# A routed mixture-of-experts block on one core: a table region per expert, slots ranked part by part, and the attention tile through the table

## The chip, the core and the metric

The kernel runs on one core of a Trainium2 chip. The metric is the device time of one execution in microseconds (us), here the median of three. In the profile, PE is TensorE (PEld its weight load), DVE VectorE, ACT ScalarE, POOL GpSimd, and SPq, ACTq, POOLq the queues of DMA-issuing or control instructions of an engine.

## What is computed

The input x has 8 sequences of 512 tokens of 256 numbers. A small attention touches only the first 16 tokens of each sequence (128 tokens in all); every token gets an output bias. Then every token goes through a router, its four best of 32 experts, and two shared experts.

```python
def reference(...):
    x = x + attn(layernorm(x))          # changes tokens 0..15 of each sequence, adds ob to all
    x = x + ffn(layernorm(x))
def ffn(tokens):                        # 4096 tokens of 256
    scores = sigmoid(tokens @ router_weight.T)             # 32 experts in 4 groups of 8
    sfc = scores + router_bias
    group_scores = top_k(grp, 2)[0].sum(-1)                # keep 2 groups, then 4 experts
    topk_w = scores[topk_idx]; topk_w = 2.5 * topk_w / topk_w.sum()
    out_e = (silu(tokens @ gate_w[e].T) * (tokens @ up_w[e].T)) @ down_w[e].T
    return sum_k(topk_w[k] * out_e[topk_idx[k]]) + shared(tokens)
```

Counting the router's choices over the given input: 16,384 pairs of a token and an expert lie on 17 experts and fill 136 tiles of 128 rows when every expert is rounded up; without the 128 attention tokens there are 15,872 pairs in 133 tiles.

## The kernel before

All in float32. Tokens lie in 32 tiles of 128: tile 0 holds the 128 attention tokens, tiles 1 to 31 the rest.

1. **Normalise and score.** DVE takes the statistics of groups of tiles (`statistics`, L1042), ACT normalises each tile (L572), PE turns it (`turn`, L730) and multiplies by the router's weights (`logits`). Turned tiles stay in SBUF as `xnT`, in the upper half of `gu_w`, where the weights of experts 16 to 31 will go.
2. **Route tiles 1 to 31** on DVE in two halves (`route_parts`, L1069): the chosen experts become a 0/1 array `hot`, PE counts with it, and DVE makes of the counts a slot in a table in DRAM for each pair. The slots of all experts are packed behind each other, each expert rounded up to 128, so a slot needs the total of every expert first.
3. **Attention** on tile 0: 23 steps that alternate between PE and DVE (`from_pe`, `to_pe`, `after_dve`), with the shared experts' work (`units`) put between them by the list `UNITS_AT`. Beside it ACT stages each tile four times with its pair numbers (`stage`, L591: 4 buffers in `xg`, so tile n waits until the rows of tile n - 4 have left), and POOL scatters four times 128 rows per tile to the table (L535), 124 times in all. `STAGE_AT` and `ADD_AT` say in which step ACT stages a tile and DVE adds a finished pair of shared-expert results to x. The table was blanked before by four DMAs of 5,140 KB (L398).
4. **Dense steps.** Tile 0 doesn't go through the table: 32 steps (`PLAN`, kind "dense") run all 32 experts over it, weighted by `w0`.
5. **Expert steps.** 134 steps (`FIXED`) load a tile of 128 rows of the table (L425, address known when the program is built), turn it (L922), gate and up (L946), turn the hidden values (L952), down (L970); POOL scatters the result to `pairs_dram` (L542). Expert numbers come from a small table read into PE registers. Steps beyond `FIXED` stand in branches that are taken only if more tiles are used (133 are).
6. **Combine.** SP loads the four results of each token (L457), DVE adds them with their weights (L1477), SP stores.

SP issues its DMAs in program order. The second half of the gate and up weights is the L418 entry below: it waits for the last `up` of the shared experts and for the 12th addition of `add_pairs`, since both still read `xnT`.

```python
            sp.wait_ge(up_done, SHARED)
            sp.wait_ge(pair_added, KEPT_IN_XNT)
            for m in range(2, 4):
                e = slice(8 * m, 8 * m + 8)
                sp.dma_start(gu_w[:, e], gate_up[:, e]).then_inc(gu_in[1], 16)
```

## Time and profile before

| | us |
|---|---|
| median of 3 runs (range) | 551.88 (550.71 to 553.16) |
| the profiled execution | 550.75 |
| its span, first to last instruction | 549.0 |
| PE busy (share of the span) | 418.3 (76%) |
| DVE, ACT, POOL busy | 280.3, 240.5, 287.9 |
| mean granted clock | 0.936 |

A row of the timeline has the start, the duration, engine, line, operation, output<-input and count, and in brackets the idle time before it and what ended it. A stretch view gives the busy time of each engine in a stretch, the granted TensorE clock as a share of 2.4 GHz, the DMA engines' share and GB/s. The chain of waits is followed back from the last instruction. All times of the trace count from the start of the span.

### The profile page before, as it was taken

To read this page: it belongs to the slowest core of one execution; us is meant where nothing else is said; L and a number is where in the kernel's file an instruction comes from. 1 tells how busy PE (TensorE), PEld (TensorE's weight loads), DVE (VectorE), ACT (ScalarE), POOL (GpSimd) and SP (SyncE) were. 2 spreads that over 40 slices of the span, in tenths; PEclk is the share of its full clock that TensorE was granted. 3 is DMA by queue.
4 is the path that set the end of the run, shared out by engine and by line. 5 is a ranking of instruction groups with operands and counts; after the bars stand their busy time and mean duration, and the time that the engine had idled before them with its cause. 6 is when DMAs were issued, how large, how long until landed. Compare 5 with 4: busy or idle time off the path is not lost.

```text
span 549.0 us, 8776 instructions
## 1 busy us (share of the span) xinstructions
PE 418.3 (76%) x2118; PEld 325.6 (59%) x2119; DVE 280.3 (51%) x997; ACT 240.5 (44%) x625; POOL 287.9 (52%) x421
## 2 busy tenths in 40 slices
PE   0699236898896976999999999999999999920000
PEld 0699114555453543888888888888888888810000
DVE  4967785764553434343366633223232322308997
ACT  0687501427644552422455555555555555510000
POOL 6430028886888888760166565656656565630000
PEclk9999998999998998999999999999999999985555
DMA  7999999532232373935055555455454454339996
GB/s 178 274 419 417 418 423 398 149 107 77 106 106 98 106 266 124 366 98 155 11 168 157 162 152 149 153 162 157 145 169 153 154 172 139 105 106 410 369 402 241
DMA packets 42549, 111.48 MB, mean 203 GB/s; under 512 B 7929, under 2 KB 25468, under 8 KB 38272
## 3 DMA queue, kind: packets, MB, share of 16 engines
q1 hardware_dynamic: 29824, 78.24, 41.5%
q0 software_dynamic: 12384, 32.59, 17.1%
q8 instruction: 23, 0.38, 0.3%
q14 instruction: 30, 0.25, 0.2%
q10 hardware_dynamic: 288, 0.03, 0.0%
HBM read 53.01 MB, written 59.13 MB: 204 GB/s over the span
## 4 chain that ended last, share of the span: by engine, by line
PE 53%; DVE 9%; ACT 2%; DMA 1%; issue 1%; SPq 0%; POOL 0%; POOLq 0%; ACTq 0%; DVEq 0%
PE two_banks L946 26%; PE two_banks L970 11%; DVE x_sb L1477 9%; PE two_banks L922 5%; PE two_banks L952 3%; PE two_banks L783 3%; PE two_banks L961 3%; PE two_banks L809 2%; DMA gu_w<-pairs_dram 1%; ACT L588 0%; ACT loopb L598 0%; DMA pairs_dram<-routing,loopb 0%; ACT routing L612 0%; PE two_banks L887 0%; PE two_banks L904 0%
## 5 line engine op out<-in xcount | busy, mean ns | idle before, releaser
L542 POOL DMA_INDIRECT pairs_dram<-routing,loopb x134 | 131.8, 984 | 112.0 <-issue 80.9
L535 POOL DMA_INDIRECT slots_dram<-loopb,slot_i x124 | 121.5, 979 | 70.6 <-DVEq L1267 41.8
L946 PE MATMUL two_banks<-gu_w,routing 128*128 x536 | 137.9, 380 | 0.0
L1439 DVE TENSOR_TENSOR routing<-routing,two_banks 128x128 f32<-128x128 f32 x134 | 38.6, 288 | 135.8 <-ACT routing L689 122.9
L946 PEld LDWEIGHTS two_banks<-gu_w,routing 128*128 128x128 f32 x536 | 91.5, 190 | 7.0
L970 PE MATMUL two_banks<-dn_w,routing 128*128 x268 | 80.0, 381 | 0.0
L684 ACT ACTIVATE routing<-two_banks 128x256 f32<-128x256 f32 x134 | 51.5, 384 | 64.9 <-PE two_banks L922 64.9
L783 PE MATMUL two_banks<-gu_w,sgu_w 128*128 128x512 f32 x128 | 64.8, 644 | 11.1 <-DMA sdn_w<-in_sh_down 5.5
L689 ACT ACTIVATE routing<-two_banks 128x128 f32<-128x128 f32 x166 | 46.1, 278 | 58.7 <-PE two_banks L946 58.7
L1477 DVE SCALAR_TENSOR_TENSOR x_sb<-gu_w,wts,x_sb 128x256 f32<-128x256 f32 x124 | 49.5, 480 | 12.7 <-DMA gu_w<-pairs_dram 12.6
L698 ACT ACTIVATE routing<-two_banks 128x256 f32<-128x256 f32 x134 | 50.6, 378 | 1.4 <-PE two_banks L970 1.3
L922 PE MATMUL two_banks<-ident,loopb 128*128 128x128 f32 x268 | 51.2, 273 | 0.0
L598 ACT ACTIVATE loopb<-x_sb,shift,rstd 128x1024 f32<-128x1024 f32 x31 | 38.2, 1233 | 27.4 <-DMA slots_dram<-loopb,slot_i 27.3
L1445 DVE COPY routing<-two_banks 128x128 f32<-128x128 f32 x166 | 47.1, 284 | 0.4 <-PE two_banks L952 0.2
L970 PEld LDWEIGHTS two_banks<-dn_w,routing 128*128 128x128 f32 x268 | 40.5, 191 | 10.3 <-issue 0.2
L783 PEld LDWEIGHTS two_banks<-gu_w,sgu_w 128*128 128x128 f32 x128 | 24.6, 205 | 36.9 <-issue 23.7
L922 PEld LDWEIGHTS two_banks<-ident,loopb 128*128 128x128 f32 x268 | 37.8, 141 | 13.5 <-issue 0.2
L952 PE MATMUL two_banks<-ident,routing 128*128 128x128 f32 x166 | 45.4, 274 | 0.3
L809 PE MATMUL two_banks<-sdn_w,loopb 128*128 128x256 f32 x128 | 32.7, 400 | 11.2 <-ACT gu_w L612 7.4
L809 PEld LDWEIGHTS two_banks<-sdn_w,loopb 128*128 128x128 f32 x128 | 24.3, 198 | 19.5 <-issue 12.5
L736 PE MATMUL two_banks<-ident,gu_w 128*128 128x128 f32 x62 | 20.5, 438 | 19.4 <-ACT gu_w L572 19.4
L946 PE MATMUL two_banks<-gu_w,xnT 128*128 128x256 f32 x128 | 32.7, 379 | 0.0
(222 smaller groups left out, 476.9 us busy)
## 6 DMA issues: line engine op xcount, KB each, us to landing
slots_dram<-gu_w SPq DMA_DIRECT2D x4, 5140.0 KB, 47.4
loopb<-slots_dram SPq DMA_DIRECT2D x134, 128.5 KB, 2.5
gu_w<-pairs_dram SPq DMA_DIRECT2D x31, 512.0 KB, 6.8
gu_w<-in_gate_up SPq DMA_DIRECT2D x4, 2048.0 KB, 12.9
out<-x_sb SPq DMA_DIRECT2D x3, 1024.0 KB
dn_w<-in_down SPq DMA_DIRECT2D x1, 2304.0 KB, 9.7
pairs_dram<-routing,loopb POOLq DMA_INDIRECT x134, 2.8
slots_dram<-loopb,slot_i POOLq DMA_INDIRECT x124, 3.2
```

Of the source, the lines that this page charges most:

```text
L535: pool.indirect_dma_start(out=slots_dram, out_offset=bass.IndirectOffsetOnAxis(ap=slot_i[:, at:at + 1], axis=0), in_=xg[:, r, 0:ROW], in_o ...
L542: pool.indirect_dma_start(out=pairs_dram, out_offset=bass.IndirectOffsetOnAxis(ap=xg[:, u % RING, D:ROW].bitcast(I32), axis=0), in_=yb[u % ...
L684: act.activation(xT[:, j % 2], turn_ps[j % 2], ACT.Copy).then_inc(xT_ready, 1)
L698: act.activation(yb[u % OUTS], y_ps(u), ACT.Copy).then_inc(y_ready, 1)
L783: ins = pe.matmul(o, weights[:, m, c, :], xnT[:, 4 * q:4 * q + 4, c, :], start=(c == 0), stop=(c == KC - 1))
L809: ins = pe.matmul(pair_y_ps[:, i, :], pair_hid[:, m, t:t + P], sdn_w[:, m, :], start=(m == 0), stop=(m == 1))
L922: ins = pe.transpose(turn_ps[j % 2][:, c, :], xg[:, u % RING, c * P:(c + 1) * P], ident[:, :])
L946: ins = pe.matmul(bank[2 + s % 2][:, 0:2 * I], rows[:, c, :], w, start=(c == 0), stop=(c == KC - 1))
L952: pe.transpose(bank[4 + s % 2][:, 0:P], hid[:, s % 2, 0:I], ident[:, :]).then_inc(hid_turned, 1)
L970: ins = pe.matmul(y_ps(n), hidT[:, s % 2, 0:P], w, start=True, stop=True)
L1445: dve.tensor_copy(hidT[:, s % 2, 0:P], bank[4 + s % 2][:, 0:P]).then_inc(hidT_ready, 1)
L1477: ins = dve.scalar_tensor_tensor(x_sb[:, m + 1, :], load4[:, m % LOADS, k, :], wts[:, m + 1, k:k + 1], x_sb[:, m + 1, :], ALU.mult, ALU.add)
```

## The change

- **Table.** Each expert gets a region of 4,224 rows (`CAP`), so a slot is the expert's first row plus the rank of the pair within its expert. No total is needed first. Slots are made in three parts (tiles 1 to 8, 9 to 16, 17 to 31) and then tile 0: `chosen` and `slots_of`, cut into seven pieces each. Part 0 runs on DVE between the statistics of the tile groups; parts 1 and 2 run inside the first ten attention steps (`ROUTE_AT`); PE's ranks are one product with a running count and one with `lower` (`rank`).
- **Blanks.** In place of the whole table only 256 rows behind each expert's last row are blanked, by 32 DMAs with an address from a register, after the counts of parts 0 to 2 are known. Scatters of tiles 1 to 31 no longer wait for the blanks, those of tile 0 do.
- **Attention tile.** The 32 dense steps are gone; tile 0 is routed, staged and scattered as the last tile. `FIXED` is 137, 136 tiles are used. Combine has 32 tiles in place of 31.
- **Order.** Four tiles are staged during the normalising (`EARLY_STAGE`); `STAGE_AT`, `ADD_AT`, `UNITS_AT` are new. The sixteen tiles of xnT in `add_pairs`: additions 10 to 15 now stand at the very end ("tail"), behind the tables.
- **Loads.** SP loads the row number of each tile from `tables` into registers, four per read, and loads a tile by register address. The first expert step waits for both halves of the gate and up weights.

```diff
+CAP = TOKENS + P
-GROUPS_OF_TILES = [(1, 5), (5, 13), (13, 22), (22, 32)]
+GROUPS_OF_TILES = [(1, 5), (5, 9), (9, 17), (17, 25), (25, 32)]
+PARTS = [(1, 9), (9, 17), (17, 32)]
-FIXED = 134
+FIXED = 137
-PLAN = [("dense", e) for e in range(E)]
+ROUTE_AT = {0: [(1, 0), (1, 1)], 1: [(1, 2), (1, 3)], 2: [(1, 4)], 3: [(1, 5), (1, 6)],
+            4: [(2, 0)], 5: [(2, 1)], 6: [(2, 2)], 7: [(2, 3)], 8: [(2, 4)], 9: [(2, 5), (2, 6)]}
+RANK_AT = {step + 1: part for step, pieces in ROUTE_AT.items() for part, piece in pieces if piece == 4}
+EARLY_STAGE = {14: 0, 18: 1, 22: 2, 26: 3}
+SCATTER_US, FIRST_US, ATT_US, STEP_US = 5.2, 47.0, 62.0, 5.5
+    _us = FIRST_US + SCATTER_US * _n - 9.6
+    _at = max(int((_us - ATT_US) / STEP_US), 0)
+    STAGE_AT.setdefault(("att", _at) if _at < ATT_STEPS else ("tail", 0), []).append(_n)
...
-            for u in range(0, SLOT_TILES // BLOCK, BLANKS):
-                sp.dma_start(slot_blocks[:, u:u + BLANKS, :],
...
+            sp.wait_ge(blanks_known, 1)
+            for first in range(0, E, 4):
+                _, starts = nc.values_load_multi_w_load_instructions(
+                    blank_at[0:1, first:first + 4], engines=(mybir.EngineType.SP,), min_val=0, max_val=SPARE - BLANK_ROWS,
...
+                for at in starts:
+                    sp.dma_start(slots_dram[bass.ds(at, BLANK_ROWS), :].rearrange("(p j) d -> p (j d)", j=2),
...
-                sp.dma_start(xg[:, u % RING, 0:ROW], slot_tiles[:, u // BLOCK, u % BLOCK, :]).then_inc(xg_in[u % RING], 16)
+                sp.dma_start(xg[:, u % RING, 0:ROW], slots_dram[bass.ds(load_row(u), P), :]).then_inc(xg_in[u % RING], 16)
+            sp.wait_ge(tables_ready, 1)
...
-            pool.wait_ge(blanked, 16 * (SLOT_TILES // BLOCK // BLANKS))
-            for n in range(TT - 1):
+            for n in range(TT):
+                t = (n + 1) % TT
+                if t == 0:
+                    pool.wait_ge(blanked, 16 * E)
+                    pool.wait_ge(slots_ready, len(PARTS) + 1)
...
+            def rank(part):
+                pe.wait_ge(hot_ready, part + 1)
+                if part < len(PARTS):
+                    a, b = PARTS[part]
+                    pe.matmul(rank_ps[part], ones_b[:, :], prefix[part][:, :, 0:b - a].rearrange("p e t -> p t e"), start=True,
+                              stop=False, skip_group_check=True)
...
+            def gate_up_of(u, eid):
+                pe.wait_ge(xT_ready, u + 1)
+                if u == 0:
                     pe.wait_ge(gu_in[0], 32)
+                    pe.wait_ge(gu_in[1], 32)
...
+                for step in range(ahead[0], pes[0]):
                     units(*UNITS_FROM[step:step + 2])
                     add_pairs("att", step)
+                    for part, piece in ROUTE_AT.get(step, []):
+                        next_of(part)
...
+            dve.tensor_scalar(tables[0:1, 2 * P:], table_ps[:, 2 * P:], float(P), None, ALU.mult).then_inc(tables_ready, 1)
+            add_pairs("tail", 0)
```

The order of the built program, at three places. First DVE in attention step 8, between the sum of the exponentials and its reciprocal. Before:

```order
L1366 TENSOR_REDUCE hst<-routing 128x16
L1143 TENSOR_TENSOR loopb<-loopb,two_banks 128x512
L1369 RECIPROCAL hst<-hst 128x16
```

The same place in the changed kernel (L1332 is the sum, L1335 the reciprocal, L1158 a unit's product, L1167 an addition to x):

```order
L1332 TENSOR_REDUCE hst<-routing 128x16
L1158 TENSOR_TENSOR loopb<-loopb,two_banks 128x512
L1167 TENSOR_TENSOR x_sb<-x_sb,gu_w 128x512
L1086 TENSOR_SCALAR small<-small 128x60
L1087 TENSOR_TENSOR routing<-routing,small 128x480
L1090 MAX top<-routing 128x8 x15
L1167 TENSOR_TENSOR x_sb<-x_sb,gu_w 128x512
L1093 MEMSET top 128x15x4
L1096 MATCH_REPLACE gu_w<-top,routing 128x32 x15
L1103 COPY gu_w<-gu_w 128x32
L1104 TENSOR_SCALAR gu_w<-gu_w 128x32x15
L1105 SCALAR_TENSOR_TENSOR gu_w<-gu_w 128x512
```

Pieces 3 and 4 of part 2 now stand there, and PE waits for the last of them (`rank(2)`) before it goes on with the attention.

Second, the end of DVE's routing of tile 0. Before, the additions to x follow at once, then the weights `w` and the first dense step:

```order
L1116 MAX top<-routing 128x8
L1118 MEMSET top 128x4
L1120 MATCH_REPLACE routing<-top,routing 128x32
L1122 TENSOR_SCALAR routing<-routing 128x32
L1152 TENSOR_TENSOR x_sb<-x_sb,gu_w 128x512
L1152 TENSOR_TENSOR x_sb<-x_sb,routing 128x512
L1401 TENSOR_TENSOR w<-routing 128x32
```

In the changed kernel, from the slots of tile 0 (L1122) over the tables of the tiles (L1373 to L1392) to the additions:

```order
L1122 TENSOR_SCALAR slot_i<-top 128x4
L1373 TENSOR_TENSOR e_row<-two_banks,next_slot 128x32
...
L1389 TENSOR_SCALAR ecol<-ecol 128x2
L1391 CAST tables<-two_banks 1x256
L1392 TENSOR_SCALAR tables<-two_banks 1x256
L1167 TENSOR_TENSOR x_sb<-x_sb,gu_w 128x512 x2
L1167 TENSOR_TENSOR x_sb<-x_sb,routing 128x512 x3
```

The 12th addition, which SP's weight load waits for, is the second of the two L1167 rows that read gu_w, behind the tables.

Third, SP's queue from the down weights to the first tiles. Before:

```order
L412 DMA dn_w<-in_down 128x4608
L418 DMA gu_w<-in_gate_up 128x4096 x2
L425 DMA loopb<-slots_dram 128x257 x17
```

Changed, each tile load with a register computation ahead of it and a read of four row numbers ahead of four tiles:

```order
L395 DMA dn_w<-in_down 128x4608
L401 DMA gu_w<-in_gate_up 128x4096 x2
L408 TENSOR_LOAD tables
L418 ISA
L418 DMA loopb<-slots_dram 128x257
```

The tile loads stand behind the second half of the gate and up weights, as before; the first PE step behind them is now an expert step.

## Rows read from the trace of the kernel before

**Rows 1.** Stretch view: start:end, length, busy us (count) per engine, clock, DMA share, GB/s.

```profile
76.00:80.00 4.00, 1.25 (x2) 0.74 (x3) 3.55 (x24) 0.00 (x0) 0.98 (x1) 1.00 1.06 430
...
196.00:220.00 24.00, 17.26 (x56) 10.13 (x55) 7.28 (x38) 10.44 (x19) 19.62 (x37) 0.93 0.64 214
246.00:262.00 16.00, 16.00 (x81) 13.72 (x80) 6.44 (x24) 3.14 (x12) 0.00 (x0) 1.00 0.48 133
262.00:484.00 222.00, 221.85 (x1225) 186.82 (x1223) 83.18 (x309) 125.78 (x403) 128.91 (x132) 1.00 0.46 144
497.00:549.00 52.00, 0.00 (x0) 0.00 (x0) 48.65 (x123) 0.00 (x0) 0.00 (x0) 0.50 0.93 353
```

**Rows 2.** Chain of waits: start, us, what; gate and up of dense and expert steps.

```profile
219.90 0.88 PE two_banks L946 x4
...
263.41 0.86 PE two_banks L946 x4
265.04 0.86 PE two_banks L946 x4
...
481.33 0.88 PE two_banks L946 x4
...
496.61 47.60 DVE x_sb L1477 x120
```

**Rows 3.** Timeline of POOL: the first scatter to the table, and the last.

```profile
79.02 1.20 POOL L535 DMA_INDIRECT slots_dram<-loopb,slot_i  x1 [41.80 <-DVEq L1267]
...
242.51 1.10 POOL L535 DMA_INDIRECT slots_dram<-loopb,slot_i  x1 [0.19 <-issue]
```

**Rows 4.** Timeline of SP's queue, and the time that the two L418 loads took to land.

```profile
216.95 0.80 SPq L418 DMA_DIRECT2D gu_w<-in_gate_up  x2
246.23 4.13 SPq L425 DMA_DIRECT2D loopb<-slots_dram  x9
...
DMA to landing us min/median/max: 10.0/13.0/16.0
```

**Rows 5.** SP's waits (us, times, longest), and its register read in the chain of waits.

```profile
SPq L415 <- DVE x_sb L1152: 21.4, 1, 21.4
...
488.95 0.48 SPq L445
```

**Rows 6.** Timeline of PE: end of the logits, start of the attention, logits of tile 0.

```profile
55.23 1.75 PE L742 MATMUL two_banks<-rt_w,gu_w 128*128 128x32 f32 x8
...
88.27 0.66 PE L826 MATMUL two_banks<-ident,routing 128*128 128x128 f32 x4 [3.85 <-DVEq L1269]
...
200.54 0.53 PE L742 MATMUL two_banks<-rt_w,xnT 128*128 128x32 f32 x4
```

**Rows 7.** Timeline of DVE: routing of the first half begins, ends; attention step 9; x of tile 0; additions.

```profile
40.68 0.66 DVE L1076 TENSOR_TENSOR routing<-routing,row_sb 128x480 f32<-128x480 f32 x1
...
51.29 0.41 DVE L1122 TENSOR_SCALAR routing<-routing 128x480 bf16<-128x480 f32 x1
...
133.20 0.41 DVE L1375 TENSOR_TENSOR routing<-routing,two_banks 128x256 f32<-128x256 f32 x1
...
191.49 0.42 DVE L1386 TENSOR_TENSOR x_sb<-two_banks,routing 128x256 f32<-128x256 f32 x1
...
216.19 0.69 DVE L1152 TENSOR_TENSOR x_sb<-x_sb,gu_w 128x512 f32<-128x512 f32 x1
```

**Rows 8.** Timeline of ACT: a staged tile; a stall on the scatters; tile 0 normalised; its scores.

```profile
57.51 1.23 ACT L598 ACTIVATE loopb<-x_sb,shift,rstd 128x1024 f32<-128x1024 f32 x1
...
166.52 1.24 ACT L598 ACTIVATE loopb<-x_sb,shift,rstd 128x1024 f32<-128x1024 f32 x1 [3.89 <-DMA slots_dram<-loopb,slot_i]
...
195.12 0.60 ACT L663 ACTIVATE at_d<-x_sb,shift,rstd 128x256 f32<-128x256 f32 x1 [1.83 <-DVE shift L1391]
...
202.76 0.18 ACT L581 ACTIVATE routing<-two_banks 128x32 f32<-128x32 f32 x1
```

**Rows 9.** Timeline of PE: eight gate and up products busy before, and after an idle stretch.

```profile
190.78 3.60 PE L783 MATMUL two_banks<-gu_w,sgu_w 128*128 128x512 f32 x8
...
208.82 5.40 PE L783 MATMUL two_banks<-gu_w,sgu_w 128*128 128x512 f32 x8 [4.24 <-ACT loopb L609]
```

**Rows 10.** DVE over the combine, from the page's list of groups.

```profile
L1477 DVE SCALAR_TENSOR_TENSOR x_sb<-gu_w,wts,x_sb 128x256 f32<-128x256 f32 x124 | 49.5, 480 | 12.7 <-DMA gu_w<-pairs_dram 12.6
```

696 lines of the change are left out of this document (327 added, 369 removed).

## The prediction, made before the changed kernel ran

> **What bounds the kernel now.** I read the stretch view first [rows 1], then the chain of waits [rows 2], then the timelines around each hand-over. From 262 to 484 us PE is busy 221.85 of 222 us at the full clock: that stage is PE's own work. The chain has the 134 expert steps from 265.04 to 481.33 [rows 2]: 133 intervals in 216.3 us, 1.63 us each. Ahead of it stand the 32 dense steps, whose first gate and up is at 219.90 and whose last at 263.41 [rows 2], 1.40 us each; the first expert step is 45.1 us after the first dense one. PE has no idle time in 246 to 262 either, though POOL has nothing to do there [rows 1]. The dense steps cover three things: the last scatter to the table, issued at 242.51 [rows 3], the first tile loads at 246.23 [rows 4], and the landing of the second half of the gate and up weights, issued at 216.95 and landed 16.0 us later, 233 us [rows 4], which only dense step 16 (at about 242) needs. Behind the expert steps comes the combine: a chain of DVE from 496.6 to 544.2 [rows 2], 480 ns an operation [rows 10]. So the question is when the first expert step can start once the cover is gone. Everything behind it is stiff.
>
> **Part 1: behind the first expert step.** Before: 549.0 - 265.04 = 284.0 us. Added: 136 used tiles and one blank one against 134, three steps at 1.63 = 4.9. One more tile in the combine: four operations; 120 take 47.60 [rows 2], so 1.6. Together 290.5. The pace stays PE's unless SP is slower than 1.63 us per tile. Its new work is a register computation per tile and a read of four numbers per four tiles. Nine loads took 4.13 us without waits, 0.46 each [rows 4]; a read on SP into a register stands at the end with 0.48, with the steps around it some 0.8 [rows 5]. A quarter of that per tile gives 0.66; if each tile paid a full one, 1.26. Both are below 1.63, and the ring is 16 deep, so I take nothing. Slower than that is rival C.
>
> **Part 2: when the scatters start and end.** Scatters now wait for the slots of part 0 alone, not for blanks and the whole count. Before, the first went at 79.02 [rows 3]. Now DVE has the scores of tiles 1 to 8 at about 30 (tile 10 of the 1.2 us pace that ends at 57 [rows 6], plus a table load). The 11.0 us that choosing took for 15 tiles (40.68 to 51.70 [rows 7]) become some 8 for eight tiles, since half of it is small operations of fixed cost. PE ranks behind turn 18, at about 42, and the slots take DVE 3 us more: first scatter at 46. 31 tiles took 79.0 to 243.6, 164.6 us or 5.3 a tile [rows 3], with stalls that came from ACT. At 5.08 to 5.3 the 31 tiles end between 204 and 210; I take 207. Tile 0's four scatters come behind that or behind its slots, 5.1 us. Blanks, 8.4 MB against 21 MB, run beside the scatters from about 120 and nobody waits for them before tile 0.
>
> **Part 3: the attention chain.** It started at 88.27 [rows 6] because all routing stood ahead of it. Now it starts when the logits end: 57 [rows 6] plus four staged tiles at 1.23 each [rows 8] and one more set of scores, so 62. Routing of parts 1 and 2 is 26 us of DVE, scaled by tiles from [rows 7] with the slots, in the first ten steps. Going through these steps one by one, with DVE's gaps there filled first: step 9 ended at 133.6 [rows 7], 45.4 after the start; now pieces 0, 1 of step 0 come behind a silu that waits for two staged tiles, piece 4 makes PE wait in step 2, pieces 3 and 4 of part 2 hold PE in step 8 for 8 us. That sums to 62 after the start, 16.6 more, so 124. About 10 of the 26 us vanish in gaps; the bounds are 0 and 26 us exposed. From step 9 to x of tile 0 took 58.3 us (133.6 to 191.9 [rows 7]), with one ACT stall on the scatters in it [rows 8]. So x of tile 0 is final at 182. ACT must also stage tiles 28 and 29 in step 22, and the latter waits for the 26th tile's scatters: 46 + 26 x 5.2 + 2.2 = 183.4, then 1.4 and a silu. ACT normalises tile 0 at 187 (before 195.12 [rows 8]). If the routing were wholly hidden, this stall would still hold it at 186; if wholly exposed, 196.
>
> **Part 4: from there to the first expert step.** Before, logits of tile 0 came 5.4 us and its scores 7.6 us after the normalising [rows 6, 8]. Then DVE's routing alternates with four units on PE (two pairs of gate and up, 3.6 us each pair [rows 9]); the last `up` ends at +13.5, slots at +16.4. Fourteen dependent table operations at some 0.2 us, PE's four small products behind two down units, two copies: tables at +21.6, that is 209. Only then come additions 10 and 11, 0.6 us each, and SP may issue the second half of the gate and up weights: +23, 210. Before, SP waited for this same addition [rows 5], which came at 216.9 [rows 7]. There 16.0 us to landing were hidden; now PE's first step waits for them, and the tile loads stand behind them in SP's queue. Bounds for the landing: 16.0 with scatters and the rest beside it, and for 4.2 MB at 430 GB/s (what the stretch 76 to 80 moved [rows 1]) 9.8; the nearest row is the measured one, but the scatters are nearly over, so I take 14. Weights at 224, tiles and first turn by then: first gate and up at 225.5. The other path, scatters to 212 or 213, 2.6 us until SP goes on (243.6 to 246.2 [rows 3, 4]), a register read, 2.5 for the load, a turn and a copy, ends at 220 and is hidden by the weights. PE has been idle for some 15 us then: after 4.24 us of idleness eight products took 5.40 in place of 3.60 [rows 9], so 2 us go to the clock. Effective start 227.
>
> By the Trainium skill, DMA: Bandwidth & Descriptors, section "Anatomy of one DMA — SWDGE (gpsimd) path", a DMA takes 2.0 us plus its bytes over 436 GB/s; for these 4.2 MB, an estimate of 11.6 us and a total 2.4 us lower than mine. The trace has 16.0 beside scatters and decides until the run shows it alone.
>
> **Sum.** 227 + 290.5 = 517.5 against a span of 549.0, 31.5 less. The profiled execution took 550.75, so 519.3; the median lies 1.1 above it, so 520.4.
>
> **Rivals.**
>
> A: the weights are not last. If the addition came earlier or they landed in 10 us, tile loads and scatters would set the start: 220, 222 with the clock, 5 less than the forecast and 515 in all; with the scatters at their shortest, 204, it is 512. For it: the two paths are 5.5 us apart. Against it: the order puts the addition behind the tables, plainly. The SBUF page speaks against it too, in a sentence to itself.
>
> By the Trainium skill, SBUF — State Buffer, section "Who interferes with whom", a DVE copy or scalar operation in a two-port mode locks GpSimd out while it runs, and GpSimd writes the scatters' descriptors. The first scatters of the trace, beside a DVE that was seldom idle, kept their pace; where the rule did bite, A would move to the forecast.
>
> B: the attention chain is later. Routing wholly exposed adds 9 us, further ACT stalls on the scatters (3.9 us each [rows 8]) a few more: normalising at 199, end at 532. For it: ACT, DVE and PE each wait in program order and the work is denser. Against: the scatters leave the same gaps.
>
> C, slower than before: SP can't keep up with register addresses. At p us a tile above 1.63, 137 tiles give 137 x (p - 1.63). It eats the whole gain from p = 1.86 on; at 2.0 the end is 571. Against it: 0.46 plus parts of 0.8 from rows. For it: no row shows a load by register address.
>
> D: the change doesn't do what it says: tile 0's scatters can't start near 207, because part 0's rank waits or the blanks are slow, and the scatter chain ends as before. Then 243.6 + 5.1 + 8 = 257 for the first step, 547.5 in span, 550 in median, no change.
>
> **Chances.** Forecast 0.60, A 0.14, B 0.18, C 0.05, D 0.03. The range of 8 in 10: A's shortest 512 less 1 is 511, B's 532 plus 2 is 534. Faster by over 0.5% (about what this measurement can tell from no change) 0.93, within it 0.02, slower 0.05.
>
> **What the profile would show.** Right: no dense step; first scatter near 46; attention's first PE step near 62; the second gate and up load issued near 210, right behind the tables, PE idle from about 208 until it lands and nothing else missing then; expert steps at 1.63; combine 1.6 longer. Wrong if PE's first expert step is released by a tile load rather than by the weights, if the attention steps take over 5.5 us on average, or if SP is busy all through the expert stage.

## The result, and the profile after

| | kernel before | changed kernel |
|---|---|---|
| median (range) of 4 runs each, us | 552.52 (550.71 to 554.17) | 527.98 (527.05 to 529.38) |
| ratio, 95% interval | | 0.9559 (0.9519 to 0.9598) |
| profiled execution / its span, us | 550.75 / 549.0 | 529.38 / 527.6 |
| first expert step's gate and up, us | 265.04 | 236.57 |
| from there to the end of the span, us | 284.0 | 291.0 |

The changed kernel is 24.5 us faster. Below, the landing of a DMA is the time from its issue to its completion. The forecast was 520.4 with a range of 511 to 534: the direction and the range held, the value was 7.6 us too low. The part behind the first expert step came out as forecast (291.0 us, where the forecast had 292.5 with the cold clock). The first expert step came 11.1 us later than forecast, 236.57 against 225.5, and for another reason than forecast: not the weights but a tile load behind the last scatter released it, which the prediction had named as a sign of being wrong. So the total lies within its range, but the path that sets the start is not the one it was forecast from.

The stretches of the changed kernel (start:end, length, busy us and count per engine in the order PE, PEld, DVE, ACT, POOL, then clock, DMA share, GB/s):

```profile
62.00:128.00 66.00, 52.91 (x215) 31.16 (x215) 48.53 (x206) 28.80 (x48) 52.73 (x95) 0.92 0.28 97
130.00:180.00 50.00, 36.58 (x184) 20.29 (x184) 24.31 (x63) 25.96 (x42) 42.63 (x79) 0.90 1.05 256
192.00:204.00 12.00, 10.06 (x35) 6.07 (x36) 3.97 (x24) 5.76 (x11) 10.11 (x20) 1.00 1.01 426
214.00:233.00 19.00, 0.00 (x0) 0.00 (x0) 3.36 (x7) 1.02 (x2) 11.25 (x16) 0.59 0.75 276
240.00:460.00 220.00, 220.00 (x1214) 185.77 (x1214) 81.98 (x304) 125.86 (x403) 130.57 (x133) 1.00 0.50 152
462.00:528.00 66.00, 0.33 (x2) 0.00 (x0) 51.02 (x128) 0.62 (x2) 2.88 (x3) 0.53 0.86 325
```

From 240 to 460 PE is as full as before [rows 1], and the pace is the same: the 137th gate and up stands at 459.29, so 136 intervals in 222.7 us, 1.64 each. New are the second row and the fourth. From 130 to 180 the DMA engines are full (a share of 1 or a little above), where the kernel before had 0.29; what has been added there are the blanks. And from 214 to 233 PE does nothing at all. What it waits for is in the chain of waits of the changed kernel (start, us, what):

```profile
212.47 1.23 ACT loopb L599
213.84 0.73 issue
214.58 1.38 POOL slots_dram L535
215.96 2.24 issue
218.20 0.12 POOL pause L538
...
226.07 6.42 DMA slots_dram<-loopb,slot_i
232.58 0.30 SPq L408
233.05 2.22 DMA loopb<-slots_dram
...
236.57 2.07 PE two_banks L923 x4
```

Read it from below: the first gate and up; the load of its tile; SP's read of the row number; the landing of the last scatter, 6.42 us; eight scatters one after another from 214.58 (those of tile 30 and of tile 0); and ahead of them not POOL but ACT, L599, the staging of tile 30. POOL had been idle before it, in its own timeline:

```profile
203.70 0.96 POOL L535 DMA_INDIRECT slots_dram<-loopb,slot_i  x1 [0.19 <-issue]
204.66 0.12 POOL L538 MEMSET pause<- 128x1 bf16 x1
214.58 3.62 POOL L535 DMA_INDIRECT slots_dram<-loopb,slot_i  x1 [9.79 <-ACT loopb L601]
```

9.79 us in which the scatters of tile 30 could have run. The staging stands in ACT's program behind all of the shared experts' units (in "tail"), and the last two are the down products of units 14 and 15:

```profile
209.23 0.60 ACT L613 ACTIVATE routing<-two_banks 128x512 f32<-128x512 f32 x1 [4.67 <-PE two_banks L795]
211.97 0.60 ACT L613 ACTIVATE loopb<-two_banks 128x512 f32<-128x512 f32 x1 [2.15 <-PE two_banks L795]
212.47 1.23 ACT L599 ACTIVATE loopb<-x_sb,shift,rstd 128x1024 f32<-128x1024 f32 x1
```

The weights are not far behind, though. SP issued the second half at 214.96, the counterpart of [rows 4]; the later of the two DMAs went out at 215.3, and if the longer landing is its own it landed 14.1 us later, at 229.4 (timeline of SP's queue, and what the view of that line says):

```profile
186.02 0.89 SPq L392 DMA_DIRECT2D gu_w<-in_gate_up  x2
192.09 0.33 SPq L395 DMA_DIRECT2D dn_w<-in_down  x1
214.96 0.80 SPq L401 DMA_DIRECT2D gu_w<-in_gate_up  x2
```

```profile
DMA to landing us min/median/max: 7.7/10.9/14.1
```

### The profile page after: what moved, and what is told of

Its sections match the earlier page's. It is cut to its first block, busy times and chain, and to the rows that moved or that the text cites. A ratio compares the mean times of both kernels' runs of the same rounds, so it can differ in the third digit from the quotient of the medians.

```text
span 527.6 us, 8705 instructions
## 1 busy us (share of the span) xinstructions
PE 384.5 (73%) x1930; PEld 296.1 (56%) x1930; DVE 268.6 (51%) x977; ACT 235.4 (45%) x604; POOL 295.1 (56%) x435
## 4 chain that ended last, share of the span: by engine, by line
PE 47%; POOL 19%; DMA 11%; DVE 9%; issue 8%; ACT 3%; SPq 1%; POOLq 0%; DVEq 0%; ACTq 0%
PE two_banks L923 23%; POOL slots_dram L535 15%; PE two_banks L940 11%; DVE x_sb L1450 7%; DMA slots_dram<-loopb,slot_i 6%; PE two_banks L909 6%; DMA gu_w<-pairs_dram 3%; PE two_banks L929 3%; POOL pause L538 2%; PE two_banks L795 2%; POOL rstd L482 2%; DMA x_sb<-in_x 1%; ACT loopb L599 1%; PE two_banks L770 1%; DVE stats L1017 1%
## 5 line engine op out<-in xcount | busy, mean ns | idle before, releaser
L542 POOL DMA_INDIRECT pairs_dram<-routing,loopb x137 | 134.8, 984 | 103.5 <-issue 82.7
L535 POOL DMA_INDIRECT slots_dram<-loopb,slot_i x128 | 127.6, 997 | 51.4 <-issue 22.6
L923 PE MATMUL two_banks<-gu_w,routing 128*128 x548 | 142.9, 384 | 0.1
L923 PEld LDWEIGHTS two_banks<-gu_w,routing 128*128 128x128 f32 x548 | 94.7, 193 | 7.9 <-issue 0.5
L682 ACT ACTIVATE routing<-two_banks 128x256 f32<-128x256 f32 x137 | 52.6, 384 | 85.9 <-PE two_banks L909 84.8
L909 PE MATMUL two_banks<-ident,loopb 128*128 128x128 f32 x274 | 53.2, 277 | 22.4 <-DMA loopb<-slots_dram 22.4
L694 ACT ACTIVATE routing<-two_banks 128x256 f32<-128x256 f32 x137 | 51.8, 378 | 1.4 <-PE two_banks L940 1.3
L687 ACT ACTIVATE routing<-two_banks 128x128 f32<-128x128 f32 x137 | 38.0, 278 | 31.7 <-PE two_banks L923 31.7
L599 ACT ACTIVATE loopb<-x_sb,shift,rstd 128x1024 f32<-128x1024 f32 x32 | 39.4, 1233 | 14.8 <-DMA slots_dram<-loopb,slot_i 14.8
L1427 DVE COPY routing<-two_banks 128x128 f32<-128x128 f32 x137 | 38.8, 283 | 0.4 <-PE two_banks L929 0.2
L929 PE MATMUL two_banks<-ident,routing 128*128 128x128 f32 x137 | 37.5, 274 | 0.1
L725 PE MATMUL two_banks<-ident,gu_w 128*128 128x128 f32 x62 | 20.5, 438 | 23.0 <-POOL gu_w L517 16.6
L795 PEld LDWEIGHTS two_banks<-sdn_w,loopb 128*128 128x128 f32 x128 | 24.8, 203 | 20.0 <-issue 14.5
L731 PEld LDWEIGHTS two_banks<-rt_w,gu_w 128*128 128x128 f32 x128 | 30.7, 329 | 0.6 <-issue 0.5
```

What stands on the lines that cost most here:

```text
L535: pool.indirect_dma_start(out=slots_dram, out_offset=bass.IndirectOffsetOnAxis(ap=slot_i[:, at:at + 1], axis=0), in_=xg[:, r, 0:ROW], in_o ...
L542: pool.indirect_dma_start(out=pairs_dram, out_offset=bass.IndirectOffsetOnAxis(ap=xg[:, u % RING, D:ROW].bitcast(I32), axis=0), in_=yb[u % ...
L599: act.activation(xg[:, r:r + TOPK, 0:D], x_sb[:, t, :].unsqueeze(1).to_broadcast([P, TOPK, D]), ACT.Identity, bias=shift[:, t:t + 1], scal ...
L682: act.activation(xT[:, u % 2], turn_ps[u % 2], ACT.Copy).then_inc(xT_ready, 1)
L694: act.activation(yb[u % OUTS], y_ps(u), ACT.Copy).then_inc(y_ready, 1)
L795: ins = pe.matmul(pair_y_ps[:, i, :], pair_hid[:, m, t:t + P], sdn_w[:, m, :], start=(m == 0), stop=(m == 1))
```

## The experiments

Line numbers shift by a few from kernel to kernel. "Tile 0" is the time at which ACT normalises it, "last scatter" the issue of its last scatter, "step 1" the first expert step's gate and up, all in us from the profile.

| kernel | median us | ratio to before (95%) | tile 0 | tables | 2nd half issued | last scatter | step 1 |
|---|---|---|---|---|---|---|---|
| changed kernel | 527.98 | 0.9559 (0.9519 to 0.9598) | 192.1 | 213.7 | 215.0 | 226.1 | 236.6 |
| stagings early | 522.21 | 0.9434 (0.9378 to 0.9490) | 194.2 | 217.2 | 218.5 | 216.3 | 232.6 |
| additions early | 524.12 | 0.9472 (0.9429 to 0.9515) | 191.5 | 214.1 | 206.1 | 225.3 | 232.0 |
| both | 522.71 | 0.9446 (0.9404 to 0.9487) | 196.7 | 219.8 | 211.8 | 218.9 | 231.7 |
| both, tile 29 late | 522.32 | 0.9441 (0.9405 to 0.9476) | 194.7 | 217.3 | 209.3 | 216.4 | 230.0 |
| that, no units ahead | 523.50 | 0.9485 (0.9468 to 0.9502) | 196.7 | 219.3 | 211.3 | 218.4 | 231.5 |
| both, weights later | 524.58 | 0.9505 (0.9488 to 0.9522) | 191.5 | 214.1 | 206.1 | 213.2 | 232.0 |
| tile 29 late, weights first | 532.60 | 0.9630 (0.9600 to 0.9660) | 194.4 | 217.0 | 224.8 | 228.4 | 245.6 |

### Stagings early

```diff
-            units(BEFORE_LOGITS, len(UNITS))
+            units(BEFORE_LOGITS, BEFORE_LOGITS + 1)
             for n in STAGE_AT.get(("tail", 0), []):
                 stage(n)
+            units(BEFORE_LOGITS + 1, BEFORE_LOGITS + 3)
             stage(TT - 1)
+            units(BEFORE_LOGITS + 3, len(UNITS))
```

> The changed kernel with one edit: ACT stages tile 30 and tile 0 between the last units (behind the silu of unit 14 and of unit 15) in place of behind all of them. In the changed kernel POOL sat idle for 9.8 us before tile 30's first scatter, and the first expert step came at 236.57, released by a tile load behind the last scatter; the second half of the gate and up weights had landed at 229.4 (issued 215.3, 14.1 us). Theory 1 (the late staging set the start): POOL runs through, last scatter issued near 214, landed by 221, and now the weights set the start: first expert step at about 230, 6 to 7 us less, 521 us in all. Theory 2 (the weights or a transfer beside them set it, the staging only filled a gap): first expert step stays within 2 us of 236.6 and the time at 526 to 528.

522.21 us: theory 1's number, and theory 2 is out. The last scatter went out 9.8 us earlier (216.3). The chain of waits now passes over the weights, as theory 1 had it, but the step came at 232.64, not 230, since they were issued later:

```profile
218.84 0.43 SPq L401
219.84 0.30 SPq L408
220.32 11.02 DMA loopb<-slots_dram
...
232.64 2.07 PE two_banks L925 x4
```

Of the 5.8 us by which the median fell, 3.9 lie ahead of the first expert step in the profiles and 1.7 behind it (289.3 in place of 291.0 us to the end of the span). The first tile load took 11.02 us, issued right behind 4.2 MB of weights in the same queue; the weights landed after 12.1. And tile 0 was normalised at 194.2, not at 192.1, with a new wait ahead of it.

### Additions early

```diff
+            add_pairs("normal", 0)
             units(UNITS_FROM[-1], BEFORE_LOGITS)
```

`"normal"` holds additions 10 and 11, which are taken out of `"tail"`.

> The changed kernel with one edit: DVE does additions 10 and 11 right behind the normalising of tile 0, before the last units, in place of behind the tables, so that SP may issue the second half of the gate and up weights when the last up is through, near 206 in place of 215. Theory 1 (the scatter chain set the start, held up by the late staging): the weights land near 220 and nobody wants them yet; the last scatter is still issued near 226, but lands without the weights beside it, in 3 in place of 6.4 us: 0 to 4 us less, 524 to 528 us. Theory 2 (the weights set the start, as I forecast): 7 to 9 us less, 519 to 521 us.

524.12 us, 3.9 less: theory 1's upper end, and theory 2, my forecast's picture, is out for this kernel. The weights were issued at 206.07, 9 us sooner, and it bought only the landing of the last scatter, 2.84 us in place of 6.42, and a little on POOL:

```profile
225.28 2.84 DMA slots_dram<-loopb,slot_i
228.21 0.29 SPq L410
```

### Both

> Both edits: tile 30 and tile 0 staged between the last units, additions 10 and 11 behind the normalising of tile 0. Theory 1 (two chains, 7 us apart, each must go): last scatter issued near 214 and landed by 218 to 221, tables at 213.7, weights at 220, first expert step at 222.5 to 225, that is 12 to 14 us less than the changed kernel, 514 to 516 us. Theory 3 (what is saved is lost to the DMA engines: 4 MB of weights now run beside eight scatters): the scatters land 8 to 14 us late and the first expert step comes at 228 or later, 519 us or more.

522.71 us: theory 1 is wrong here. The gains of 5.8 and 3.9 us don't add up; both edits together give 5.3. Theory 3's number fits, and the profile shows two places. In the chain of waits of this kernel, ahead of tile 0 and at the end:

```profile
185.67 9.22 DMA slots_dram<-loopb,slot_i
...
218.89 8.76 DMA slots_dram<-loopb,slot_i
227.74 0.30 SPq L410
```

The first is ACT, which stages tile 29 in attention step 22 and must wait until tile 25's rows have left; behind that staging stands the normalising of tile 0:

```profile
195.00 1.24 ACT L601 ACTIVATE loopb<-x_sb,shift,rstd 128x1024 f32<-128x1024 f32 x1 [6.84 <-DMA slots_dram<-loopb,slot_i]
```

In the changed kernel the same wait was 1.33 us (ACT at 188.80). There the blanks were through at 186 and the first half of the weights was issued behind tile 25's last scatter (184.70); here they were through at 182.6, and 4.2 MB of weights were issued 3 us ahead of that scatter.

### Tile 29 late, and no units ahead of the attention

```diff
             keep_turned(TT - 1)
+            stage(29)
```

Tile 29 is taken out of the list of attention step 22.

> The version with both edits, and tile 29 staged behind the normalising of tile 0 in place of in attention step 22. In that version ACT's staging of tile 29 waited 9.2 us for tile 25's last scatter to land (185.7 to 194.9), so tile 0 was normalised at 196.8, against 192.1 in the changed kernel, and everything behind it moved 4.7 us. Theory 4 (ACT's stagings tie the attention chain to the landing of the scatters, and what the two edits saved went into that wait): tile 0 normalised at 190 to 192, weights issued at 205 to 206, last scatter issued near 214, first expert step at 223 to 226 against 231.7: 6 to 8 us less than with both edits, 515 to 517 us. Rival (Theory 3, the DMA engines are the bound: the bytes of blanks, weights and scatters must pass in any order): tile 0 is normalised sooner but the scatters or weights land only at 228 or later, first expert step at 230 or more, 521 us or more.

522.32 us, no gain over "both": theory 4 is wrong, the rival's numbers came (521 or more, step at 230). Tile 0 came at 194.7. The wait for tile 25 was gone, but an earlier staging waited 1.67 us (for a scatter issued at 173.40 that landed 9.07 us later), where it had waited 0.49 in "both", and PE then ran its next gate and up products at a granted clock of 0.66 (185 to 190; 1.00 in the changed kernel): four of them took 2.77 us in place of 1.88. The last scatter, issued at 216.39, took 9.59 us beside the second half of the weights. The stretch view of this kernel:

```profile
140.00:180.00 40.00, 25.79 (x135) 14.22 (x134) 16.42 (x41) 21.27 (x34) 34.17 (x63) 0.87 1.04 257
192.00:222.00 30.00, 19.39 (x70) 10.78 (x68) 15.72 (x75) 11.78 (x20) 19.84 (x38) 0.96 1.00 352
```

From 192 to 222 the DMA engines are at a share of 1.00 too.

Then, on top of it, the two units that stand ahead of the first attention step moved into steps 5 and 6:

```diff
-UNITS_AT = [2, 2, 2, 2]
-UNITS_AT += [2, 2, 2, 3, 1, 1]
+UNITS_AT = [0, 2, 2, 2]
+UNITS_AT += [2, 3, 3, 3, 1, 1]
```

> The version with tile 29 staged late, and no shared-expert units ahead of the first attention step on PE (they took 6.24 us at a low clock in the changed kernel, 62.06 to 68.14; two units stand in steps 5 and 6 more). Theory A (the attention chain is a chain: what it starts earlier it ends earlier): first attention step at 62 to 63, tile 0 normalised at 186 to 187, tables and last up 5 us earlier; but the scatters (128 at 1.27 us from 46.5, last issued at 214) then set the start, first expert step at 221 to 223: 2 to 3 us less than without this edit. Rival (the steps are paced by units, routing and stagings, and the later steps fill up): tile 0 normalised at 190 or later, no gain, within 1 us.

523.50 us, no gain: the rival. The attention began at 63.0 in place of 68.1, and its step 9 ended on DVE at 132.6, in place of 129.9 in the changed kernel and 128.4 in the version that this run builds on. What was taken out ahead of the steps was paid within them. The work of the two units was moved here, not saved.

### Weights later

```diff
+            sp.wait_ge(norm_ready, len(GROUPS_OF_TILES) + 1)
             for m in range(2):
                 e = slice(8 * m, 8 * m + 8)
                 sp.dma_start(gu_w[:, e], gate_up[:, e]).then_inc(gu_in[0], 16)
-            sp.wait_ge(norm_ready, len(GROUPS_OF_TILES) + 1)
```

> The version with both edits (tile 29 still staged in attention step 22), but SP issues the first half of the gate and up weights behind the normalising's statistics of tile 0 (near 192) in place of at 182.6, right behind the blanks. It asks what made tile 25's last scatter take 9.2 us to land. Theory 4a (those 4 MB beside it): it lands in under 5 us, ACT normalises tile 0 by 192, last scatter issued near 214; then 10.5 MB of weights pass between 192 and 220, and the first expert step comes at 226 to 230 against 231.7. Rival 4b (the blanks' own backlog): the landing stays near 9 us, tile 0 at 196 to 197, first expert step at 231 or later.

This separates the two halves of the question. Theory 4a is right on the cause: with no weights beside it, ACT's wait for tile 25 is gone, tile 0 stands at 191.5, the tables at 214.1, the last scatter is issued at 213.22, the earliest of all. And it buys nothing, 524.58 us, for the last scatter now needs longer than ever:

```profile
213.22 14.75 DMA slots_dram<-loopb,slot_i
```

The weights put off are still to be passed, 10.8 MB from 191.6 on, and from 192 to 222 the engines moved 395 GB/s at a share of 0.99. Its step at 232.0 is later than the 226 to 230 that I expected. The engines had room that it didn't use: from 180 to 190, with the first half of the weights put off, their share was 0.44.

### Without the second half, and larger pieces for the blanks

These three ran on one chip on which the kernel before took 627.28 us and the waits ahead of the expert steps are longer; only their times and rows against each other are read. All three are the version with tile 29 late and one edit; that version itself was not run on this chip. The first leaves out the load of the second half of the weights; the other two write the same blank rows in larger pieces:

```diff
-                sp.dma_start(gu_w[:, e], gate_up[:, e]).then_inc(gu_in[1], 16)
+            sp.sem_inc(gu_in[1], 32)
```

```diff
-                    sp.dma_start(slots_dram[bass.ds(at, BLANK_ROWS), :].rearrange("(p j) d -> p (j d)", j=2),
-                                 blank[:, :, :].rearrange("p j d -> p (j d)")).then_inc(blanked, 16)
+                    sp.dma_start(slots_dram[bass.ds(at, BLANK_ROWS), :].rearrange("(p j) d -> p (j d)", j=8),
+                                 blank[0:BLANK_ROWS // 8, :, :].rearrange("p j d -> p (j d)")).then_inc(blanked, 16)
```

> The version with tile 29 staged late, without the second half of the gate and up weights (4.2 MB); it leaves out the weights of experts 16 to 31, so those experts work with other numbers. It asks what the first expert step still waits for when this load costs nothing. In that version the last scatter was issued at 216.4 and SP went on only at 226.5; tables at 217.3. Theory 6 (the last scatters land late because the weights pass beside them): SP goes on by 220, first expert step at 222 to 224 in place of 230.0, 514 to 517 us. Rival (the scatters' landing is long from blanks and first weights, or of itself): first expert step at 227 or later, 519 us or more.

> The version with tile 29 staged late, its 256 blank rows per expert written as 64 pieces of four rows (4,112 bytes) in place of 128 pieces of two (2,056 bytes); same bytes, same addresses. In the profile of that version the DMA engines are busy from 130 to 180 at a share of 1.05 but move only 247 to 271 GB/s, where the whole-table blanks of the kernel before (40 KB pieces) and its scatters moved 417 to 423. Theory 5 (the engines' time goes by the pieces, and the engines are the bound from 130 to the first expert step): the blanks are through 10 us or more earlier, the first weights are issued by 172 in place of 183.7, the scatters land in 3 to 5 us, tile 0 is normalised by 192, the second half of the weights issued by 206, first expert step at 223 to 226 in place of 230.0: 515 to 518 us. Rival (the bytes count, or the writes to these rows as such, whatever the pieces): no change, 521 to 523 us.

> The same with 32 pieces of eight rows (8,224 bytes) per expert. Theory 5: at least as early as with four rows, first weights issued by 165, first expert step at 222 to 225, 514 to 517 us. Rival (bytes): no change, 521 to 523 us.

592.52, 596.40 and 596.10 us; ratios 0.9472 (0.9396 to 0.9548), 0.9491 (0.9446 to 0.9537) and 0.9440 (0.9375 to 0.9506), which overlap. The times alone don't tell them apart, and by them the gain of 5 us or more that theory 6 expected isn't there: the ratio without the second half is no lower than that of tile 29 late on the other chip (0.9441). What is left are the rows of one profile each. With the second half (pieces of eight rows), the chain of waits has

```profile
285.12 8.60 DMA slots_dram<-loopb,slot_i
293.81 0.29 SPq L411
```

and without it SP's read stands at 288.38, with the last scatter issued at 285.14, nearly the same time. What released the read is not the scatter but DVE's tables:

```profile
287.96 0.40 DVE tables L1397
...
288.38 0.30 SPq L409
...
292.23 1.96 PE two_banks L927 x4
```

So without the weights the last scatter was in by 288.36, 3.2 us after its issue at most, and with them it took 8.60: 4.2 MB beside it cost it 5.4 us or more, in two profiles that differ in the size of the blank pieces too. The first expert step came 5.5 us sooner (292.23 against 297.73), and then it was the tables that held it. Theory 6 is borne out for the landing; for the time of the kernel it isn't shown.

On the size of the pieces theory 5 is wrong, the rival right. From the first blank's issue to the first weights behind the blanks took 50.8 us with two rows a piece (173.0 to 223.8), 53.6 with four (171.6 to 225.2) and 52.5 with eight (171.3 to 223.8). The profile with four rows is of its longest run, 603.69 us. While the blanks run, in 192 to 222, the stretches are, two rows, four rows and eight rows a piece, in this order:

```profile
192.00:222.00 30.00, 15.89 (x64) 8.64 (x64) 8.11 (x17) 10.62 (x18) 17.42 (x32) 0.72 1.04 247
```

```profile
192.00:222.00 30.00, 13.18 (x56) 6.63 (x56) 6.31 (x12) 10.29 (x17) 17.17 (x32) 0.69 0.93 232
```

```profile
192.00:222.00 30.00, 14.08 (x57) 7.54 (x58) 5.82 (x13) 9.93 (x16) 17.22 (x33) 0.68 0.95 238
```

247 at a share of 1.04, 232 at 0.93, 238 at 0.95: about 240 to 250 GB/s for a full share, with any of the three.

### Weights first

```diff
+            sp.wait_ge(xn_turned, TT - 1)
+            for m in range(2):
+                e = slice(8 * m, 8 * m + 8)
+                sp.dma_start(gu_w[:, e], gate_up[:, e]).then_inc(gu_in[0], 16)
             for first in range(0, E, 4):
...
-                    sp.dma_start(slots_dram[bass.ds(at, BLANK_ROWS), :].rearrange("(p j) d -> p (j d)", j=2),
-                                 blank[:, :, :].rearrange("p j d -> p (j d)")).then_inc(blanked, 16)
+                    sp.dma_start(slots_dram[bass.ds(at, BLANK_ROWS), :].rearrange("(p j) d -> p j d", j=2),
+                                 blank[:, :, :].to_broadcast([P, 2, ROW])).then_inc(blanked, 16)
```

> The version with tile 29 staged late, and SP issues the first half of the gate and up weights ahead of the blanks (near 127) in place of behind them (183.7); for that the blank row has a tensor of its own, one row wide, and is written as 1,028-byte pieces. All bytes stay. In that version the DMA engines are busy at a share of 0.8 to 1.1 from 130 to 220, and the first expert step at 230.0 waits for the last scatter's landing (issued 216.4, SP goes on at 226.5) beside the second half of the weights (209.3 to 225.1). Theory 7 (the DMA engines bound the stretch; what passes at 250 GB/s with the blanks is not lost, and 4 MB fewer stand between the blanks and the tables): blanks are through by 185 to 195, the second half is issued at 206 to 209 and lands by 222, the last scatter lands within 6 us, first expert step at 224 to 227: 516 to 519 us. Rival A (the bound is one of order, not bytes: ACT's stagings now wait for scatters that land beside weights and blanks from 130 on): attention steps later, tile 0 normalised after 196, 522 us or more. Rival B (the last scatters' landing is slow because of the second half alone): first expert step within 1.5 us of 230.0, 521 to 523 us.

532.60 us, worse than the changed kernel. Only rival A's number covers it, and not its mechanism (tile 0 at 194.4). What the rows point to is the size of the pieces, which I had thought a detail. In 1,028-byte pieces the blanks took from 130 to 224 (the second row is SP issuing them):

```profile
128.43 0.82 SPq L386 DMA_DIRECT2D gu_w<-in_gate_up  x2
130.13 84.00 SPq L392 DMA_DIRECT2D slots_dram<-blank  x32
224.39 0.34 SPq L397 DMA_DIRECT2D dn_w<-in_down  x1
```

and the stretch 192 to 222, long after the weights that stand ahead, moved 192 GB/s at a share of 0.97. Now tile 0's scatters wait for the blanks (12.6 us), and everything queued on SP behind them too. So smaller pieces went with a lower rate, and larger ones gave nothing. Whether the order of weights and blanks matters this run doesn't tell, since both edits are in it.

### The dense steps alone, and a read per tile

The kernel before with its plan cut to the expert steps; it leaves out the experts' part for tile 0. The stagings and additions that stood among the dense steps come behind the last units:

```diff
-PLAN = [("dense", e) for e in range(E)]
+PLAN = []
```

> The kernel before without its 32 dense steps, the stagings and additions that stood among them moved to the end of the units; it leaves out the experts' part for tile 0. It asks how much of the gain is the dense steps alone. Theory 1 (without cover the scatters set the start): last scatter issued at 242.5 as before, first expert step at about 250 in place of 265, behind it 284 us unchanged: span 534, 536 us in all, 16 us less; so the region table with its early scatters is worth the other 9 us and pays for three more expert steps too. Rival (the dense steps cost nearly all of 45 us, the scatters speed up without their traffic): first expert step at 240 or before, 526 us or less. Rival 2 (the scatters wait for stagings that stood among the dense steps): no gain, 545 us or more.

537.31 us, ratio 0.9712 (0.9670 to 0.9754): theory 1 within 1.3 us. The last scatter in the chain of waits, and the first expert step in PE's timeline:

```profile
243.80 2.94 DMA slots_dram<-loopb,slot_i
```

```profile
250.70 1.91 PE L946 MATMUL two_banks<-gu_w,routing 128*128 x4
```

So taking out 45 us of dense work is worth 15.6 us. The region table and the new order together moved the first expert step by another 14.1 us (250.7 to 236.6), of which 4.9 go to three more expert steps. The parts add up to the whole: 15.6 + 14.1 - 4.9 = 24.8, measured 24.5.

The changed kernel with a register read for each tile on SP, 137 reads in place of 35:

> The changed kernel with SP reading the row number of each tile by a read of its own, 137 reads in place of 35. It measures how far SP is from setting the pace of the expert stage. By the rows of before a load with its register computation takes 0.46 us and a full read 0.5 to 0.8, together 1.26 us a tile at most, below PE's 1.63: no change, 526 to 529 us, with the pace of the steps at 1.63. Rival (a read costs SP over 1.2 us, for it must wait for its value): the pace goes above 1.63 us and the run takes 535 us or more.

One run of 528.36 us, within the 526 to 529 expected, and PE full in the stretch view:

```profile
240.00:460.00 220.00, 220.00 (x1216) 185.47 (x1214) 82.19 (x305) 126.13 (x404) 130.94 (x133) 1.00 0.52 153
```

SP is not near its limit in the expert steps.

## Why the prediction was right or wrong

**Right: part 1.** 291.0 us from the first expert step to the end, forecast 292.5 with the clock. The pace is 1.64, register addresses cost nothing (rival C is out, even with four times the reads). The idle PE lost some 1.4 us to the clock: the first two intervals took 4.63 (236.57 to 241.20), at a granted clock of 0.50, in place of 3.3; I had 2. One more combine tile cost 0.6 rather than 1.6 (last expert step's end to the end of the span: 462.3 to 527.6, before 484.4 to 549.0).

**Right: the first scatter and the length of the attention steps.** First scatter at 46.51 (forecast 46). PE was held 6.4 us by `rank(2)` where I had 8. From the attention's first PE step to the end of step 9, read on DVE as in [rows 7], 61.7 us (forecast 62), and from there to x of tile 0 59.0 (forecast 58.3).

**Right: part 4's chain.** From the normalising of tile 0 (192.10): logits +5.4, scores +7.6, last `up` +13.5, slots +16.1, tables +21.6, weights issued +22.9; forecast +5.4, +7.6, +13.5, +16.4, +21.6, +23. The landing was 14.1 us (I took 14). The Trainium skill, DMA: Bandwidth & Descriptors, "Anatomy of one DMA — SWDGE (gpsimd) path", gave an estimate of 11.6 for them; its fit is for DMAs that GpSimd issues, and these go out on SP's queue. Where only tile loads ran beside them (stagings early) the trace has 12.1, near it; beside scatters it has 14.1 to 19.4, and there it doesn't hold.

**Off by 5: tile 0, through the start of the attention.** Normalised at 192.1, forecast 187. The attention's first PE step came at 68.14, not 62: two units stand ahead of it, 6.24 us on PE, a row of the list `UNITS_AT` that I had not costed. As the two lengths above were right, all of this arrived at the end: step 9 ended at 129.9 (forecast 124) and x of tile 0 was final at 188.9 (182). From DVE's timeline and ACT's in the changed kernel:

```profile
129.47 0.41 DVE L1341 TENSOR_TENSOR routing<-routing,two_banks 128x256 f32<-128x256 f32 x1
...
188.46 0.42 DVE L1352 TENSOR_TENSOR x_sb<-two_banks,routing 128x256 f32<-128x256 f32 x1
```

```profile
192.10 0.60 ACT L664 ACTIVATE at_d<-x_sb,shift,rstd 128x256 f32<-128x256 f32 x1 [1.33 <-DVE shift L1357]
```

The last row is the normalising of tile 0: ACT, done with its stagings, waited 1.33 us for DVE. The staging of tile 29, which I had let go at 183.4 and took for what holds this step, went at 188.80, but it was not what held it here; it was in "stagings early" and "both", where x of tile 0 was final at 187.7 and 189.6 and tile 0 normalised at 194.2 and 196.7. Moving the two units into steps 5 and 6 gave nothing back; leaving their work out wasn't tried.

What I also missed there is the DMA engines. The median landing of the scatters to the table rose from 3.2 us to 6.4, and the chain has 8.26 us for the one issued at 173.33. My sentence "Blanks, 8.4 MB against 21 MB, run beside the scatters from about 120 and nobody waits for them before tile 0" was true only of their own semaphore: with the scatters beside them they fill the engines for 50 us (256 GB/s at a share of 1.05), and ACT's stagings wait for scatters that land late. In the changed kernel the steps behind step 9 still took only 0.7 us more than I had.

**Wrong: part 2 and "the other path ends at 220 and is hidden".** It ended at 236.6, and it is the term that made the forecast too low. Of 16.6 us, 9.6 are POOL's idle time before tile 30: I let tile 0's scatters follow "behind that or behind its slots" and went by POOL's pace, and did not go through ACT's order of that stretch, where `STAGE_AT` puts tile 30 into "tail" behind the last two down units. Another 2.7 are one scatter of 3.62 us, 2.8 the longer landing of the last one (6.5 us from its issue to SP's read, before 3.7 [rows 3, 4]), and the remaining 1.5 are the pace and the steps behind the landing. The staging as the cause of the idle time is shown (stagings early: last scatter 9.8 us sooner, 5.8 us gained). The weights were 5 us late as well, like tile 0; had the scatters ended in time, they would have set the start at about 231 (an estimate: 229.4 and the 1.5 us that I had from there), so both paths of the forecast were too short and the one I took as hidden by more.

**What replaced it.** My rival A had this mechanism (weights not last) with the sign turned: I priced it as a gain. What the forecast lacked altogether is the DMA engines as a resource of the stretch. Seven arrangements with two-row blanks put the last scatter anywhere between 213 and 226, the weights between 206 and 219 and tile 0 between 191 and 197, and six of them have step 1 between 230.0 and 232.6.

Why it stays there is shown in part. In "both", "tile 29 late" and "no units ahead" the last scatter, issued while the second half of the weights was under way, landed 0.5 to 0.7 us after it (by the longest landing of the weights, at 227.0, 225.4 and 226.9), and step 1 came 4.0 us behind that landing. So an earlier scatter gains nothing there: it comes in with the weights. "Weights later" is the same with more bytes: 10.8 MB from 191.6 on, the engines at 0.99 from 192 to 222, the weights in at 225.9 and the scatter at 228.0. Taking the 4.2 MB away made the last scatter land sooner (5.4 us or more, in one pair of profiles).

That the bytes of 130 to 225 as a whole set the 230 is not shown, and for two kernels the stretch views speak against it. In the changed kernel the engines had room just ahead of the weights:

```profile
210.00:220.00 10.00, 2.90 (x16) 1.97 (x16) 5.35 (x16) 3.05 (x5) 5.05 (x5) 0.87 0.44 158
```

and in "stagings early" they had 0.39 in the same ten us. There the weights simply were issued late, behind the tables. A run without the blanks, which would show their part, was not made, since the table would hold undefined numbers.

**The chances.** Faster had 0.93. The range's upper end was set for a late attention chain (rival B). That lateness came, 5 us, from units ahead of the chain rather than from exposed routing or stalls of ACT, and the larger part of the miss came from the scatters; that the total stayed in the range is owed to the width left for B, not to a forecast of what happened. Rival D didn't come: the first scatter went out at 46.51.

The better version is "stagings early" or "both, tile 29 late", 522.2 and 522.3 us: ratios 0.9434 and 0.9441 to the kernel before, about 1% below the changed kernel. The runs don't tell them from each other.

## What to carry to other kernels

When a cover of work is taken away, follow every engine's program order through the uncovered stretch, not only the pace of the engine that issues last: the wait that set the end here was an ACT step placed by a table of numbers. Look at the share of the DMA engines and at what is under way when the last small DMA is issued: where 4.2 MB of weights were, it landed with them, however early it had gone out. And an early start of a chain is worth only what its last feeder (staging, slots, weights, blanks) lets through: the first scatter went 32.5 us sooner than before (46.51 against 79.02), the last of now 128 only 16.4 (226.07 against 242.51).

## What the runs showed of the hardware

**A scatter beside additions of DVE took longer.** In the changed kernel the first scatter of tile 30 took 3.62 us on POOL, the median is 0.96. It ran beside seven additions of DVE without a gap, timelines of DVE and POOL:

```profile
213.61 1.27 DVE L1167 TENSOR_TENSOR x_sb<-x_sb,gu_w 128x512 f32<-128x512 f32 x2
214.81 1.88 DVE L1167 TENSOR_TENSOR x_sb<-x_sb,routing 128x512 f32<-128x512 f32 x3
...
216.95 0.41 DVE L1170 TENSOR_TENSOR x_sb<-x_sb,loopb 128x256 f32<-128x256 f32 x1
```

```profile
218.20 0.12 POOL L538 MEMSET pause<- 128x1 bf16 x1
```

The additions end at 217.36 and the scatter at 218.20, 0.84 later. With two additions fewer (additions early) they end at 216.56 and the scatter, of 2.42 us, at 217.39, 0.83 later; in the run with a read per tile the two ends are 217.85 and 218.69. I had discounted this. The Trainium skill, SBUF — State Buffer, "Who interferes with whom", says that a DVE instruction with two SBUF inputs contends with GpSimd's reads from SBUF, and infers that `tensor_tensor` leaves the generation of descriptors alone; the first agrees with these three pairs of ends. Whether the scatter waited with its reading of the slots from SBUF or with its descriptors the rows don't tell, so the second stays open for it. A single addition cost little: in the kernels whose last additions met no scatter (stagings early, both), the longest scatter was 1.61 us.

**Blanks are slow for their bytes.** 256 rows at 32 places, beside scatters: about 240 to 250 GB/s at a full share, whether in pieces of 2, 4 or 8 KB, and just under 200 in 1 KB pieces, where weights beside scatters moved 426 (192 to 204) and the whole-table blanks of the kernel before 424 (66 to 70). Those had no scatter beside them, for the first one waited for them; the stretch 76 to 80 [rows 1] has the first weights in it, issued at 76.81. The scatters get slower beside the blanks too: from 90 to 120 they moved 2.76 MB for 25.9% of the engines, 355 GB/s at a full share, and from 135 to 160 2.25 MB for 35.5%, 253 GB/s (both estimates from these numbers). What slows them is open.

**The landing of a scatter** depends on what is under way near it: 2.5 us at the least, a median of 2.6 from 90 to 120, 8.8 to 9.6 beside 4.2 MB of weights, 14.75 behind 8.4 MB and more. The profile has the two in different queues, on the same 16 DMA engines; that the engines are what they wait for is inferred from that.
